# A two-layer decoder on one core: four small steps of a hand-written schedule are moved by one or more slots

## What is computed

```python
x = x + _L0_attn_ref(_layernorm(x), ...)                       # token mixing, gates and a decaying scan over tokens
x = x + _L0_xattn_ref(_layernorm(x), ctx_1024, ctx_1024, ...)   # 16 heads of 64, 128 keys of ctx and 128 memory keys
x = x + _L0_ffn_ref(_layernorm(x), ...)                         # router, the best 2 of 8 experts, gelu

# in _L0_xattn_ref
q = queries @ wq_w + wq_b
k = concat(keys @ wk_w + wk_b, mk)
attn = softmax(q @ k.T / sqrt(64));  out = attn @ v @ wo_w + wo_b

# in _L0_ffn_ref
router_logits = einsum('bth,eh->bte', x, router_w)
topk_values, topk_indices = top_k(router_logits, 2)
```

## Time and profile before

| | |
|---|---|
| median of 3 runs | 1462.2 us (1461.46 to 1464.87) |
| the profiled execution's own time | 1474.45 us |
| its span | 1472.2 us |
| slots 0 to 127 of the first phase | 112.2 to 756 us of the span |
| PE busy, by the page | 1313.6 us, 89% |
| DVE busy | 1124.6 us, 76% |
| ACT busy | 1090.5 us, 74% |
| POOL busy | 594.1 us, 40% |
| mean granted TensorE clock | 0.971 |

### The profile page before, as it was taken

How to read it: one execution, slowest core, us unless ns; L and a number is a source line. 1 busy time by engine, 2 the same in 40 slices (tenths; PEclk the granted TensorE clock), 3 DMA queues, 4 the chain that set the end, 5 groups by cost and what they waited for, 6 DMA issues and landing times.

```text
span 1472.2 us, 42907 instructions
## 1 busy us (share of the span) xinstructions
PE 1313.6 (89%) x15449; PEld 965.4 (66%) x15449; DVE 1124.6 (76%) x2733; ACT 1090.5 (74%) x2900; POOL 594.1 (40%) x679
## 2 busy tenths in 40 slices
PE   4358999999999999999974999888989999999994
PEld 1125666667676666677663999756667777777763
DVE  6998889999998988876654344367688888787765
ACT  2128999999999999999971666557767777877763
POOL 0012424343534434310115553346655665545552
PEclk9999999999999999999995999889999999999997
DMA  6942242423322242030112332220101010000000
GB/s 146 245 119 55 54 95 52 116 58 81 79 61 71 59 105 55 9 87 6 48 37 63 107 91 65 89 92 18 28 13 38 12 40 12 22 24 3 24 10 15
DMA packets 82300, 88.49 MB, mean 60 GB/s; under 512 B 15536, under 2 KB 71472, under 8 KB 77488
## 3 DMA queue, kind: packets, MB, share of 16 engines
q1 hardware_dynamic: 78000, 77.36, 20.2%
q0 software_dynamic: 4096, 8.40, 2.0%
HBM read 64.76 MB, written 17.83 MB: 56 GB/s over the span
## 4 chain that ended last, share of the span: by engine, by line
PE 64%; DVE 16%; ACT 10%; issue 7%; DMA 1%; POOL 1%; SPq 0%; another core or an unknown queue 0%; ACTq 0%; DVEq 0%; POOLq 0%
PE P L756 7%; PE P L2026 7%; PE P L915 6%; PE P L1511 4%; PE P L1544 4%; PE P L897 3%; PE P L773 3%; ACT pr L967 3%; PE P L874 3%; PE P L2044 3%; PE P L885 3%; PE P L869 3%; PE P L2087 3%; PE P L1977 2%; DVE xnE L2346 2%
## 5 line engine op out<-in xcount | busy, mean ns | idle before, releaser
L967 ACT ACTIVATE pr<-P,nm 128x256 f32<-128x256 f32 x512 | 239.1, 500 | 6.0 <-DVE nm L1153 6.0
L1153 DVE TENSOR_REDUCE nm<-P 128x4 f32<-128x1024 f32 x128 | 156.1, 1219 | 26.0 <-PE P L756 23.8
L2230 ACT ACTIVATE et<-P 128x1024 f32<-128x1024 f32 x128 | 131.2, 1025 | 46.1 <-PE P L2033 45.0
L756 PE MATMUL P<-kt_w,qt 64*128 64x256 f32 x1024 | 145.4, 402 | 4.6 <-ACT pr L967 4.6
L352 POOL TENSOR_TENSOR rstd<-ve,mhalf 128x1 f32<-128x1 f32 (+2 forms) x81 | 73.3, 908 | 184.3 <-DVE ve L347 183.7
L951 ACT COPY ptS<-P 128x512 f32<-128x512 f32 x256 | 138.1, 599 | 7.5 <-PE P L773 7.1
L942 ACT ACTIVATE pr<-pr,ri 128x256 f32<-128x256 f32 x256 | 120.4, 536 | 24.5 <-DVE pr L1126 23.9
L1603 ACT ACTIVATE hT<-P,mixing 128x128 f32<-128x128 f32 x284 | 81.3, 369 | 66.9 <-PE P L1511 57.6
L674 POOL TENSOR_TENSOR kv_qk<-kv_qk,mixing 128x512 f32<-128x512 f32 x48 | 61.1, 1273 | 150.8 <-DVE pr L1126 150.8
L668 POOL TENSOR_TENSOR kv_qk<-kv_qk,r_w 128x512 f32<-128x512 f32 x48 | 61.0, 1272 | 145.3 <-DVE pr L1126 99.7
L967 ACT ACTIVATION_READ_ACCUMULATOR pr<-P,nm 128x1 f32 x512 | 118.4, 231 | 0.0
(11 more groups left out here) (350 smaller groups left out, 3803.7 us busy)
## 6 DMA issues: line engine op xcount, KB each, us to landing
kv_qk<-scr_v SPq DMA_DIRECT2D x16, 1024.0 KB, 8.0
r_w<-scr_r SPq DMA_DIRECT2D x16, 1024.0 KB, 10.6
xt<-scr_xs SPq DMA_DIRECT2D x71, 64.0 KB
scr_ys<-yt SPq DMA_DIRECT2D x71, 64.0 KB
x<-in_x SPq DMA_DIRECT2D x8, 256.0 KB, 10.3
scr_v<-mixing SPq DMA_DIRECT2D x8, 256.0 KB, 2.4
scr_r<-mixing SPq DMA_DIRECT2D x8, 256.0 KB, 2.0
xb<-in_x SPq DMA_DIRECT2D x8, 256.0 KB, 3.4
```

The lines of the kernel that those rows point to most:

```text
L756: m = nc.tensor.matmul(scores(s)[:, hh, cc * KEYS:(cc + 1) * KEYS], QT[part, c, b * T:(b + 1) * T], keys, start=True, stop=True)
L967: e = nc.scalar.activation(pr[:, s % 3, h * KEYS:(h + 1) * KEYS], scores(s)[:, h // 2, (h % 2) * KEYS:(h % 2 + 1) * KEYS], ACT.Exp, bias=n ...
L1153: nc.vector.tensor_reduce(nm[:, s % 3, 0:4].rearrange("p (a h) -> p a h", a=2), scores(s).rearrange("p a (h k) -> p a h k", k=KEYS), AX.X, ...
L2230: nc.scalar.activation(et[:, u % 4, :, :, :], scoresT, ACT.Exp).then_inc(S["h_exp"], 1)
```

## The change

Four things are moved; no instruction is added or taken away. `xt` goes from offset -7 to -6 (slot 9 of a group to slot 10). `cxt`, `lg` and `order` of the groups 0 to 6 go one slot on: slots 11, 12 and 13 (the two halves of group 7 keep theirs). The first eight chunks of queries and keys, which alternated in pairs (keys 0, 1, queries 0, 1, keys 2, 3, queries 2, 3), now come as four of the keys and then four of the queries. And the queries' layernorm does two sequences in DVE's slot 8 and two in its slot 9.

```diff
@@ -72,7 +72,7 @@
 BANK7 = {"norm": -45, "dd": -44, "v": -36, "r": -35, "k": -33, "w": -32, "g": -24, "o": -15, "og": -11, "out": -9,
-         "xt": -7, "cxt": 26, "lg": 27, "cum": 30}
+         "xt": -6, "cxt": 27, "lg": 28, "cum": 30}
@@ -165,10 +165,10 @@
-CHAIN = {"eps": 25, "xn": 25, "cxt": 26, "lg": 27, "order": 28, "sel": 29, "tanh": 30, "cum": 30, "base": 31, "slot": 32}
+CHAIN = {"eps": 25, "xn": 25, "cxt": 27, "lg": 28, "order": 29, "sel": 29, "tanh": 30, "cum": 30, "base": 31, "slot": 32}
...
-CHAIN_SECOND_HALF = {**CHAIN, "eps": 24, "xn": 26}
+CHAIN_SECOND_HALF = {**CHAIN, "eps": 24, "xn": 26, "cxt": 26, "lg": 27, "order": 28}
@@ -530,7 +530,11 @@
             def qk_chunk(s):
                 g, k = divmod(s + 8, SLOTS)
-                return (g, 2 * (k // 4) + k % 2, k % 4 < 2) if 0 <= g < GROUPS else None
+                if k < 8:
+                    chunk = (g, k % 4, k < 4)
+                else:
+                    chunk = (g, 2 * (k // 4) + k % 2, k % 4 < 2)
+                return chunk if 0 <= g < GROUPS else None
@@ -1243,7 +1247,10 @@
-                        ln_tails(dve, 1, ALL, xb[:, g % 3, :, :], xn, "b_rs", g + 1, "b_xn")
+                        ln_tails(dve, 1, ALL[:2], xb[:, g % 3, :, :], xn, "b_rs", g + 1, "b_xn")
+                    g = group_at(s, -7)
+                    if g is not None:
+                        ln_tails(dve, 1, ALL[2:], xb[:, g % 3, :, :], xn, "b_rs", g + 1, "b_xn")
```

## The result

The changed kernel takes 1497.64 us (median of 4 runs, 1494.76 to 1501.47) where the kernel before takes 1463.53 on the same chip (4 runs, 1461.46 to 1465.63): ratio 1.0245, 95% interval 1.0226 to 1.0265. That is 34.1 us slower; forecast were 30.9, 1493.1 us with a range of 1476 to 1504.

The account below looks back on a forecast made before the run. PE's amount of work was taken to set the pace in the slots. Waits of 4.1 + 13.9 + 4.7 + 3.7 = 26.4 us plus 4.5 of clock, 30.9, on 1462.2 gave 1493.1 us, range 1476 to 1504.

Parts of the forecast that it names:

- Layernorm: Slots 57 and 58: layernorm over two slots, transposes one on; PE waits 1.03 us more a group, 4.1 us for four.
- Keys ahead: Keys' chunks ahead of queries': costs nothing, up to 0.2 us either way a group.
- Logits: Slots 28, 44, 60, 76: logits wait for ACT's copy of the values product, 3 x 3.65 and 2.93, 13.9 us.
- Comparisons: Slot 62 and its like in the first four groups: PE waits 1.17 us for DVE's later read, 4.7 us.
- Later groups: Three groups without a values product (slots 94, 110, 126): waits from comparisons and layernorm, together 3.7 us.
- The clock: PE falls to the lower clock behind the three gaps of 3.65 us, 1.5 us each, 4.5 us.
- the upper bound of 12: Upper bound of the clock term: 4 x 3.0 us for falls of twice the length in all four gaps.
- (a): Waits without the clock, PE being dense on both sides of single gaps: 26.4 us, 1488.6; chance 0.27.
- (b): A long fall of 17.1 us in each of the four groups: 7.5 us each, 30 us, 1518.6; chance 0.06.
- (c): Half hidden: DVE meets POOL at other times, ACT's copy comes a microsecond sooner; about 14 us, 1476; chance 0.12.
- (d): Faster: DVE's relief in slot 8 removes the 0.94 us wait ahead of 773 in six groups, 5.6 us, 1456.6; chance 0.03.
- (e): No change: engines drift apart and absorb the waits, or the logits' move has no effect in steady slots; 1462; chance 0.05.

Follow-up runs that it names:

- the experiment: Changed kernel with all four operations of the queries' layernorm in DVE's slot 8 again, transposes still in slot 10: ratio 1.0244.
- products in the gap: Changed kernel with unread PE products between the mixer's values product and the logits in slots 28, 44, 60, 76: six, ratio 1.0217; three, 1.0170.
- the trace with ACT's copy moved: Changed kernel with ACT copying the mixer's values product ahead of its four exponentials instead of behind them: ratio 1.0120, 17.7 us slower than before.
- the runs that did remove it: Kernel before, scan of slot 7 behind the values' read: ratio 1.0014; scans of 9 and 13 too: 0.9996; slot 7 with POOL's power first: 0.9994.
- the comparisons alone: Kernel before with only the comparisons (order) one slot on, logits and their transposes staying: ratio 1.0057, 8.4 us slower.
- the router's steps alone: Kernel before with only the router's three steps (cxt, lg, order) one slot on: ratio 1.0222, 33 us slower.
- the logits first: Changed kernel with PE's logits ahead of the mixer's values product and DVE's copy of them behind its maxima: ratio 1.0150, 22 us slower than before.

## Why the prediction was right, and where it was off

The mechanism was the forecast's, at the places it named: the logits behind ACT's copy in slots 28, 44, 60 and 76 and not in 92 and 108; line 777 of slot 58 later by 0.53 us against its slot 57; slot 62 held by the comparisons. The groups were to take 91.6 us and took 91.4, 92.5, 91.6. The total came out at 34.1 us for 30.9. Step by step, in the traces:

- *Layernorm*: 1.03 us of waiting a group were forecast. Slots 9 and 10 took 10.54 us for 10.03 with the transposes of 0.49 gone to the later of them and the router's gone from it: 1.00. Right, and the experiment puts 0.5 of it on the two operations.
- *Keys ahead*: nothing, and nothing it was.
- *Logits*: 3.65 us three times and 2.93 once, 13.9, were forecast. The logits start 5.87 and 5.50 us into slot 12, where they could at 2.52 (the start of PE's next product behind the mixer's, before and with products in the gap): 3.35 and 2.98, 13.0 us. The step that failed is that the copy's time would hang on DVE's scaling alone and stay where it was when slot 59 got shorter. In slot 60 before, the exponentials started behind ACT's own copies, not behind DVE's maxima (ACT, then DVE):

```profile
426.48 1.05 ACT L951 COPY ptS<-P 128x512 f32<-128x512 f32 x2
427.42 0.48 ACT L967 ACTIVATE pr<-P,nm 128x256 f32<-128x256 f32 x1
...
425.81 1.21 DVE L1153 TENSOR_REDUCE nm<-P 128x4 f32<-128x1024 f32 x1
```

  After, the maxima start at 441.86, 2.17 us into the slot instead of 1.78, and the exponentials at 3.41 instead of 3.39, now behind the maxima. The copy ends 5.82 us into the slot, before 5.81. So the 0.4 us that slot 59 got shorter were not lost here.
- *Comparisons*: 1.17 us in slot 62; 1.12, and another 0.13 in slot 63, 4.9 us for 4.7.
- *Later groups*: 3.7 us forecast, 1.6 + 0.4 - 0.1 = 1.9 between the traces. But slots 98 to 100 and 113 to 116 take 31.7 us together in this trace and 33.0 to 33.4 in all the others, before and after the change; these 1.5 us are no part of the mechanism, and what made them is not known. Without them it is 3.5, and 3.6 in the trace with ACT's copy moved, which has the same steps there. The comparisons cost 1.27, 0.86 and 0.68 us in slots 94, 110 and 126 (2.8 for 2.5); the layernorm 0.4 in each of two groups, for 0.94 and 0.25.
- *The clock*: this is the term that was mis-sized. 4.5 us were forecast (three falls of 3.4 us); all four waits came with a fall, of 3.4, 6.8, 3.4 and 6.8 us. Against 3.87 us from the logits to the slot's end at full clock, with three products in the gap, they cost 1.6, 2.7, 1.6 and 2.9 us, 8.8: about twice the term. Left out were the fourth fall and the doubled length of two; the upper bound of 12 was the nearer one. The Trainium skill's remark that every turn of such a loop starts cold ("TensorE: Matmul & The Clock Gate", "HAM oscillation — how this bites in real kernels") was taken for 1.5 us more. The traces agree that a fall comes with each of the four waits, the one of 2.8 us included, but not that PE always starts cold: in slots 28 and 60 the logits ran at full clock and it fell 1.5 and 1.8 us behind their start.

4.0 + 13.0 + 4.9 + 1.9 + 8.8 = 32.6 us, for 32.8 between the traces' slots. That the total is so close is luck in part: 4.3 us too little clock stand against 1.1 us too much waiting (25.3 for 26.4) and the 1.5 us that the seven later slots were shorter. The 1.3 us between 32.8 and the 34.1 of the medians are within the spread of the runs.

The rivals: (a), waits without the clock, is what three products in the gap make of it, 1.0170 or 25 us for the 26.4 worked out. (b) was not seen: no fall in the slots lasted over 6.8 us, where the one behind the slots had lasted 17.1. (c) fell, DVE met POOL as before (the two scalings of slot 60 take 1.64 us, before 1.65). (d), relief reaching back to slot 8: PE's wait there is 0.78 us as it was 0.77, and the runs that did remove it gained nothing. (e) fell with the first of the rows.

## What to carry to other kernels

When a step of a software pipeline moves into another slot, ask what else in that slot uses the same buffer and who empties it, in its own program order: here one bank with a reader at the end of its slot cost about 3 us each time, and putting the reader ahead of its engine's other work took half of the whole loss back. Price a long wait of TensorE with the time at half clock that comes with it: here each of the 16 waits of 2.5 to 3.3 us in four traces had such a fall, and in the changed kernel the falls added some 70% to the waits themselves. And where three engines are each over 90% busy, removing one wait is no gain until the next delivery of the same engine is looked at: three attempts here only moved it.

## What the runs showed that was not expected

- The clock falls behind short idle times too, and not every time. 1.72 us idle in slot 94 was followed by a fall in three traces (the comparisons alone, the router's steps alone, the layernorm in one slot) and by none in the five others that have it, the changed kernel's among them; 1.6 us in slot 126 by one in three of nine; 0.91 us, with the logits first, was followed by one in slot 44 and by none in slots 28 and 60 of the same execution.
- With the same wait of 3.19 us a fall lasted 3.4 us in some groups and 6.8 in others, and most of the longer ones began before the wait was over, so slot 12 took from 11.3 to 12.8 us. With three products in the gap the four slots are equal to 0.01 us but for slot 76, whose copy is earlier. Whether this is what spreads the changed kernel's runs by 6.7 us (the kernel before: 4.2) is not shown: the slower runs had the lower mean granted clock (1494.76 us at 0.970, 1501.47 at 0.965), but with the three products they still spread by 5.8.
- The chips of the experiments ran the kernel before in 1474 us where the first one ran it in 1463. The changed kernel's trace, from the first chip, is 9 to 13 us shorter between slot 127 and line 2040's first product with `kTe` than all the others, so the 11 us are behind the slots. What it is in that stretch was not tried.
